# Perceiver block on one core: expert weights summed by accumulating DMAs, the key split on GpSimd, all query copies on ScalarE, new instruction orders

## The chip, the cores and the metric

The kernel runs on one core of one Trainium2 chip. Its engines are TensorE (PE; PEld are its weight loads), VectorE (DVE), ScalarE (ACT), GpSimd (POOL) and SyncE (SP, which here only issues DMAs). The metric is the device time of one execution in microseconds (us).

## What is computed

A batch of 64 x 64 tokens of width 128 goes through a cross attention on a context, a causal attention over binary trees, and a layer of product-key experts, each with a layer norm ahead and a residual sum behind.

```python
def reference(x, ctx_768, ...):
    x = x + _L0_xattn_ref(_layernorm(x), ctx_768, Wq, Wk, Wv, Wo, bo)   # 16 heads of 64
    x = x + _L0_attn_ref(_layernorm(x), Wp, bp, Wv, Wo)                 # 16 heads, tree depth 5
    x = x + _L0_ffn_ref(_layernorm(x), Wq, bq, K1, K2, W_up, W_down)    # 8 heads, 32 x 32 keys, top 10
    return x

def _L0_ffn_ref(x, ...):
    q = (x @ Wq + bq).reshape(B, S, N_HEADS, D_QUERY)
    s1, s2 = einsum(q[..., :16], K1), einsum(q[..., 16:], K2)
    v1, i1 = top_k(s1, 10); v2, i2 = top_k(s2, 10)
    vals, best = top_k((v1[..., :, None] + v2[..., None, :]).reshape(..., 100), 10)
    expert_idx = take_along_axis(i1[..., :, None] * 32 + i2[..., None, :], best)
    scores = softmax(vals)
    h = gelu(einsum('bsd,bshkd->bshk', x, W_down[expert_idx])) * scores
    return einsum('bshk,bshkd->bsd', h, W_up[expert_idx])
```

## The kernel before, in words

**Tiles.** The tokens are cut into 32 tiles of 128 (two sequences each). Every tile goes through over 100 steps; a step has a name such as `x.s0` and is a handful of instructions of one engine. The prefix tells the part: `x.` and `y.` are the cross attention, `t.` the tree attention, `k.` the keys, `e.` the experts.

**Order.** Each engine runs through `for i in range(NT + depth)` and, in each iteration, through its own table (`PE_ORDER`, `ACT_ORDER`, `DVE_ORDER`, `POOL_ORDER`, `SP_ORDER`) from first name to last. The number at a name is its lag: in iteration `i` the step works on tile `i - lag`, so that about five tiles are under way at once. An engine never leaves its table's order: what waits holds up all behind it. Between engines every step waits on semaphores, one for each name (`s[name]`, counted per tile). `BANK` says in which bank of PSUM a step of PE writes: x0, x1, t0, t1 are single banks, f0 and f1 are double ones that the experts use in turn.

**Cross attention.** `x.norm` (POOL) and `x.turn` (PE) give the transposed input; `x.q0` to `x.q3` make the queries of four heads each, `x.w0` to `x.w3` copy them to SBUF (L622 on ACT, `x.w3` L626 on DVE); `x.s0` to `x.s3` are the scores, `x.x` their maxima (DVE), `x.e` the exponentials (ACT, L694), `x.r` the reciprocals (DVE), `x.n` the scaling (POOL, L1057), `x.p` the transposes, `x.t` their copies, `y.m` the mixes, `y.u` their copies, `y.out` the projection, and `y.res` the residual sum with the statistics of the next layer norm (DVE, L893).

**Trees.** `t.norm` (POOL, L1044 and L1047), `t.turn`, `t.sb`, `t.pv`, `t.pexp`, `t.path`, `t.feat` (POOL), `t.fturn`, `t.fsb`, `t.sim`, `t.exp`, `t.mix`, `t.div`, `t.cturn`, `t.csb`, `t.out`, `t.res`: one dependent chain over all engines.

**Keys.** `k.norm`, `k.turn`, `k.high`/`k.low`, then `k.key` gives the scores of 16 x 32 keys. `k.top` (DVE) takes the eight largest of each key list and subtracts the largest in place in PSUM. `k.split` (DVE, L950 and L952) writes the shifted scores as two float16 parts into `us`; `k.kturn` (SP) turns `us` with a transposing DMA into `usT`. `k.shift` (ACT, L755) copies the shifted scores into `cand`; in this kernel it waits for `k.split`. `k.inner` (POOL) adds the inner candidates. `k.cand` (DVE, three groups of eight) finds the threshold, `k.cut` (POOL) its middle, `k.eb`, `k.z` and `k.lnz` the logarithm of the softmax's sum.

**Experts.** For each of 8 heads `h`, `e.s<h>` (PE, L589) expands `usT` to the sums of all 1024 experts, `e.x<h>` (ACT, L784) takes their exponential, `e.w<h>` (DVE, L996) masks it into one of four slots of `mw`. `e.a1` to `e.a7` (POOL, L1117) add the eight masked arrays one after another into `wsum`, 128 x 1024 float32 each. `e.wturn` transposes `wsum`, `e.hid` and `e.gelu` are the hidden values, with an activation table loaded before and after the Gelu, `e.gate` (DVE, L1007) multiplies the two, `e.out` and `e.add` finish the tile.

**Setup.** Some products of weights are made once: `setup_vo` on PE ahead of the first `x.s0`, `setup_keys` on PE ahead of the first `x.p1`. Their weights lie in buffers of their own.

## Time and profile before

| | us |
|---|---|
| median of 3 runs | 1101.47 |
| lowest and highest | 1100.77 and 1102.71 |
| the profiled execution's own time | 1100.73 |
| its span | 1097.8 |
| busy PE, share of the span | 980.3, 89% |
| busy POOL | 892.2, 81% |
| busy DVE | 876.6, 80% |
| busy ACT | 873.4, 80% |

The profiled execution lies 0.7 us under the median. The busy times are sums over the whole span; PE's matmuls are pipelined and their ends are modelled, so that its busy share is an upper estimate of its work. All four engines are busy for most of the span, and none for all of it. Except for the filling and the emptying of the pipeline the program repeats one iteration, so its trace is best read as one period.

### The profile page before, as it was taken

To read this page: it belongs to the slowest core of one execution; us is meant where nothing else is said; L and a number is where in the kernel's file an instruction comes from. 1 tells how busy PE (TensorE), PEld (TensorE's weight loads), DVE (VectorE), ACT (ScalarE), POOL (GpSimd) and SP (SyncE) were. 2 spreads that over 40 slices of the span, in tenths; PEclk is the share of its full clock that TensorE was granted. 3 is DMA by queue.
4 is the path that set the end of the run, shared out by engine and by line. 5 is a ranking of instruction groups with operands and counts; after the bars stand their busy time and mean duration, and the time that the engine had idled before them with its cause. 6 is when DMAs were issued, how large, how long until landed. Compare 5 with 4: busy or idle time off the path is not lost. (4 is left out here: it accounts for less than half of the span.)

```text
span 1097.8 us, 35846 instructions
## 1 busy us (share of the span) xinstructions
PE 980.3 (89%) x12440; PEld 778.7 (71%) x12440; DVE 876.6 (80%) x2877; ACT 873.4 (80%) x2127; POOL 892.2 (81%) x935
## 2 busy tenths in 40 slices
PE   6879899999999999999999999999999999999765
PEld 5667677777777777777777777777777777777533
DVE  3267888888888888888888888888888888888773
ACT  3548888888888888888988888888888888988652
POOL 1327888898888888988888898888888988888765
PEclk9979999999999999999999999999999999999876
DMA  6000011110100111100011110100111100010000
GB/s 166 14 19 17 12 26 26 26 26 20 24 16 20 27 25 26 26 20 14 20 26 26 26 26 20 24 14 23 26 26 26 25 21 15 20 24 20 14 13 5
DMA packets 70367, 27.25 MB, mean 25 GB/s; under 512 B 47312, under 2 KB 69936, under 8 KB 70192
## 3 DMA queue, kind: packets, MB, share of 16 engines
q1 hardware_dynamic: 69152, 24.58, 9.6%
q8 instruction: 103, 1.69, 0.6%
q14 instruction: 72, 0.59, 0.2%
q10 hardware_dynamic: 1040, 0.39, 0.1%
HBM read 14.47 MB, written 2.10 MB: 15 GB/s over the span
## 5 line engine op out<-in xcount | busy, mean ns | idle before, releaser
L1117 POOL TENSOR_TENSOR wsum<-wsum,mw 128x1024 f32<-128x1024 f32 x192 | 452.8, 2358 | 5.5
L996 DVE SCALAR_TENSOR_TENSOR mw<-psF,cut,ew 128x1024 f32<-128x1024 f32 x256 | 324.9, 1280 | 46.0 <-ACT ew L784 46.0
L784 ACT ACTIVATE ew<-psF,lnz 128x1024 f32<-128x1024 f32 x256 | 280.9, 1124 | 12.5 <-PE psF L589 9.7
L1057 POOL TENSOR_TENSOR p<-p,rrow 128x512 f32<-128x512 f32 x128 | 131.5, 1038 | 94.0 <-DVE rrow L882 94.0
L694 ACT ACTIVATE p<-psXT,negmax 128x128 f32<-128x128 f32 x512 | 181.4, 383 | 2.2 <-DVE negmax L873 2.2
L589 PE MATMUL psF<-sel,usT 128*128 128x512 f16 x512 | 158.8, 394 | 18.0 <-DVE mw L996 16.6
L377 PEld LDWEIGHTS psXT<-cT,q 96*128 96x128 f32 x1024 | 131.4, 194 | 54.8 <-DVE q L626 39.8
L377 PE MATMUL psXT<-cT,q 96*128 96x128 f32 x1024 | 142.3, 283 | 27.7 <-DVE q L626 25.6
L694 ACT ACTIVATION_READ_ACCUMULATOR p<-psXT,negmax 128x1 f32 x512 | 115.4, 225 | 0.0
L873 DVE TENSOR_REDUCE negmax<-psXT 128x4 f32<-128x512 f32 x128 | 85.9, 671 | 35.3 <-PE psXT L377 35.3
L418 PE MATMUL psXT<-pT,c 128*32 128x384 f32 x768 | 104.4, 499 | 0.7 <-ACT pT L622 0.7
L420 PE MATMUL psXT<-pT,c 128*32 128x128 f32 x768 | 102.5, 277 | 0.0
L312 PE MATMUL psXT<-xnT,qk 128*96 128x128 f16 x512 | 91.1, 222 | 3.4 <-DVE xnT L864 1.8
L439 PE MATMUL psXT<-vo,uT 128*128 128x128 f32 x768 | 92.6, 277 | 0.0
L1047 POOL TENSOR_SCALAR xn<-x,mv,rstd 128x128 f32<-128x128 f32 x96 | 76.9, 801 | 17.3 <-POOL rstd L1044 17.3
L313 PE MATMUL psXT<-xnT,qk 128*96 128x128 f16 x512 | 90.7, 221 | 0.0
L314 PE MATMUL psXT<-xnT,qk 128*96 128x128 f16 x512 | 90.7, 221 | 0.0
L439 PEld LDWEIGHTS psXT<-vo,uT 128*128 128x128 f32 x768 | 88.3, 192 | 0.0
L1044 POOL TENSOR_TENSOR rstd<-mv,halfneg 128x1 f32<-128x1 f32 x96 | 54.2, 564 | 37.1 <-DVE mv L850 34.6
L755 ACT ACTIVATE cand<-psXT 128x512 f32<-128x512 f32 x32 | 19.1, 597 | 80.9 <-DVE us L952 80.9
L1117 POOL TENSOR_TENSOR wsum<-mw 128x1024 f32<-128x1024 f32 x32 | 75.6, 2361 | 8.9 <-DVE mw L996 8.9
L622 ACT ACTIVATE pT<-psXT 128x512 f32<-128x512 f32 x128 | 74.1, 605 | 9.6 <-PE psXT L396 8.8
(133 smaller groups left out, 2359.7 us busy)
## 6 DMA issues: line engine op xcount, KB each, us to landing
cT<-cT_dram SPq DMA_DIRECT2D x32, 96.0 KB, 2.0
c<-c_dram SPq DMA_DIRECT2D x32, 96.0 KB, 2.1
x<-x_dram SPq DMA_DIRECT2D x32, 64.0 KB, 2.3
xr<-x_dram SPq DMA_DIRECT2D x32, 64.0 KB, 1.8
y_dram<-y SPq DMA_DIRECT2D x32, 64.0 KB, 1.6
wqT<-wqT_dram SPq DMA_DIRECT2D x1, 512.0 KB, 5.0
wo<-wo_dram SPq DMA_DIRECT2D x1, 512.0 KB, 6.2
wdT<-wdT_dram SPq DMA_DIRECT2D x1, 512.0 KB, 3.5
```

What stands on the lines that cost most here:

```text
L312: pe.matmul(out, left[:, 0, :], right[:, 0, :], start=not open_group, stop=False)
L313: pe.matmul(out, left[:, 0, :], right[:, 1, :], start=False, stop=False)
L377: mm = pe.matmul(bank[BANK[f"x.s{k}"]][:, i * M:i * M + M], q[:, b, h:h + 2, :].rearrange("c h q -> c (h q)"), cT[:, t % 2, b, :], start=T ...
L418: pe.matmul(to[32 * j:32 * j + 32], cols, probs[:, :, 0:3, :], start=True, stop=True, tile_position=(0, 32 * j))
L420: mm = pe.matmul(to[96:128, :, j, :], cols, probs[:, :, 3, :], start=True, stop=True, tile_position=(0, 96))
L439: mm = pe.matmul(out, uT[:, i, :, :].rearrange("c b q -> c (b q)"), vo[:, i, :], start=False, stop=(i == XH3 - 1))
L589: mm = pe.matmul(bank[BANK[f"e.s{h}"]][:, j * 512:j * 512 + 512], usT[:, t % 4, h, :], sel[:, j * 512:j * 512 + 512], start=True, stop=True)
L694: ins = act.activation(p[:, k, i, :], bank[BANK[f"x.s{k}"]][:, i * M:i * M + M], ACT.Exp, bias=negmax[:, k, i:i + 1], accum_out=rowsum[:, ...
L784: done(f"e.x{h}", act.activation(ew[:, h % NEW, :], bank[BANK[f"e.s{h}"]], ACT.Exp, bias=lnz[:, t % 4, h:h + 1]))
L996: done(f"e.w{h}", dve.scalar_tensor_tensor(out=mw[:, h % NMW, :], in0=bank[BANK[f"e.s{h}"]], scalar=cut[:, t % 4, h:h + 1], in1=ew[:, h % ...
L1057: done(f"x.n{k}", pool.tensor_tensor(p[:, k, :, :], p[:, k, :, :], rrow[:, k, :].unsqueeze(2).to_broadcast([128, 4, M]), ALU.mult))
L1117: done(f"e.a{h}", pool.tensor_tensor(wsum[:, t % 2, :], mw[:, 0, :] if h == 1 else wsum[:, t % 2, :], mw[:, h % NMW, :], ALU.add))
```

## The change

The change has five parts.

1. **Sums of the weights.** `mw` has twelve slots where it had four (`slot(t, h)` walks round them). Six of the seven additions leave POOL's arithmetic: three accumulating DMAs, issued by POOL (`e.sa`, `e.sb`, `e.sc`), each add two neighbouring slots (128 x 2048 float32, 1 MB) onto the tile's first two. Each waits for the one before to land. `e.fin` adds the last two slots on POOL into `wsum`. POOL itself waits where a DMA has to have landed.
2. **Key split.** `k.split` moves from DVE (two instructions from PSUM) to POOL (three instructions from `cand`). So it now waits for `k.shift`, and `k.shift` waits for `k.top` only.
3. **Query copies.** `x.w3` moves from DVE to ACT.
4. **Setup.** `setup_vo` now stands ahead of the first `x.p0` and `setup_keys` ahead of the first `t.turn`; their weights are loaded into `mw` slots 5 to 11, which are free until tile 0 or 1 masks into them. `setup_vo` has one wait for all its products on ACT where it had four.
5. **New tables.** All five orders and the banks are new, with the semaphore waits for the banks that follow from them. All lags but those of a few steps at the table's ends are one less; the distances between steps are about the same.

```diff
-NEW, NMW = 4, 4
+LOWEST = -16.0
+NEW, NMW = 4, 12
+SUMS = ("e.sa", "e.sb", "e.sc")
...
+        mw = sb("mw", [128, NMW, NE])
+
+        def early(i, at, parts, n):
+            return mw[0:128, i, at:at + parts * n].rearrange("p (h d) -> p h d", h=parts)
+
+        wdT = mw[:, 5, :]
+        fwqT, fbqT, keys = early(6, 0, 2, D), early(6, 256, 2, 96), early(6, 512, 4, 2 * NSQ)
...
+        def slot(t, h):
+
+            return (FH * t + h) % NMW
...
             def w_turn(t):
-                after(pe, "e.w3", t + 1)
+                after(pe, "e.w0", t + 1)
                 at_ends(pe, "e.add", t - 1)
-                pe.wait_ge(s[f"e.a{FH - 1}"], t + 1)
+                pe.wait_ge(s["e.fin"], t + 1)
...
             def shifted(t):
-                act.wait_ge(s["k.split"], t + 1)
+                act.wait_ge(s["k.top"], t + 1)
                 after(act, "k.cand", t - 2)
+                after(act, "k.split", t - 2)
...
-            def split(t):
-                dve.wait_ge(s["k.top"], t + 1)
-                after(dve, "k.kturn", t - 1)
-                lsp.begin(t)
-                uh = bank[BANK["k.key"]].rearrange("p (h i) -> p h i", h=FH)
-                lsp.link(dve.tensor_scalar_max(us[:, :, 0, :], uh, FLOOR))
-                lsp.wait()
-                done("k.split", dve.scalar_tensor_tensor(out=us[:, :, 1, :], in0=uh, scalar=FLOOR, in1=us[:, :, 0, :],
-                                                         op0=ALU.max, op1=ALU.subtract))
...
-                    if h < NMW:
-                        after(dve, f"e.a{h + FH - NMW}", t - 1)
-                    else:
-                        dve.wait_ge(s[f"e.a{max(h - NMW, 1)}"], t + 1)
-                    done(f"e.w{h}", dve.scalar_tensor_tensor(out=mw[:, h % NMW, :], in0=bank[BANK[f"e.s{h}"]],
+
+                    after(dve, ("e.sb", "e.sc", "e.fin", "e.sa")[h // 2], t - (2 if h < 4 else 1))
+                    done(f"e.w{h}", dve.scalar_tensor_tensor(out=mw[:, slot(t, h), :], in0=bank[BANK[f"e.s{h}"]],
...
+            def split(t):
+
+                pool.wait_ge(s["k.shift"], t + 1)
+                after(pool, "k.kturn", t - 1)
+                lsp.begin(t)
+                pool.nop(nofuse=True)
+                scores = cand[:, t % 2, :, 0:2 * NSQ]
+                lsp.link(pool.tensor_scalar_max(us[:, :, 0, :], scores, FLOOR))
+                lsp.wait()
+                lsp.link(pool.tensor_tensor(rest[:], scores, us[:, :, 0, :], ALU.subtract))
+                lsp.wait()
+                done("k.split", pool.tensor_scalar_max(us[:, :, 1, :], rest[:], LOWEST))
+            steps["k.split"] = split
...
-                    done(f"e.a{h}", pool.tensor_tensor(wsum[:, t % 2, :],
-                                                       mw[:, 0, :] if h == 1 else wsum[:, t % 2, :],
-                                                       mw[:, h % NMW, :], ALU.add))
...
+            def add_pairs(name, h, before):
+
+                def step(t):
+                    for i in range(h if before else 0, h + 2):
+                        pool.wait_ge(s[f"e.w{i}"], t + 1)
+                    if before:
+                        pool.wait_ge(s[before], 16 * (t + 1))
+                    pool.nop(nofuse=True)
+                    to, by = slot(t, 0), slot(t, h)
+                    pool.dma_start(mw[:, to:to + 2, :], mw[:, by:by + 2, :], accum_op=ALU.add).then_inc(s[name], 16)
+                return step
+            steps["e.sa"] = add_pairs("e.sa", 2, None)
+            steps["e.sb"] = add_pairs("e.sb", 4, "e.sa")
+            steps["e.sc"] = add_pairs("e.sc", 6, "e.sb")
+
+            def add_last(t):
+                pool.wait_ge(s["e.sc"], 16 * (t + 1))
+                after(pool, "e.wturn", t - 2)
+                done("e.fin", pool.tensor_tensor(wsum[:, t % 2, :], mw[:, slot(t, 0), :], mw[:, slot(t, 1), :], ALU.add))
+            steps["e.fin"] = add_last
...
 POOL_ORDER = {
-    "e.a7": 6, "k.cut": 5, "x.norm": 2, "t.feat": 4, "x.n0": 3, "x.n2": 3, "e.a1": 5, "x.n1": 3, "x.n3": 3,
-    "e.a2": 5, "k.norm": 4, "e.a3": 5, "e.a4": 5, "e.a5": 5, "k.inner": 4, "e.a6": 5, "t.norm": 3,
+    "e.sc": 5, "k.cut": 4, "t.feat": 3, "x.norm": 1, "x.n0": 2, "e.fin": 5, "e.sa": 4, "x.n2": 2, "x.n1": 2,
+    "x.n3": 2, "k.norm": 3, "e.sb": 4, "k.inner": 3, "k.split": 3, "t.norm": 2,
 }
...
-PE_VO = "x.s0"
-PE_KEYS = "x.p1"
+PE_VO = "x.p0"
+PE_KEYS = "t.turn"
```

**POOL, second half of an iteration, before.** From `k.norm` to `k.cut`; the name in brackets is the semaphore that a row waits for (`e_a5` is the fifth addition, `y_res` the residual sum that `t.norm` needs).

```order
L1047 TENSOR_SCALAR xn<-x,mv,rstd 128x128 [waits pool_k_norm]
L1117 TENSOR_TENSOR wsum<-wsum,mw 128x1024 [waits e_w3,e_a2]
L1117 TENSOR_TENSOR wsum<-wsum,mw 128x1024 [waits e_w4,e_a3]
L1117 TENSOR_TENSOR wsum<-wsum,mw 128x1024 [waits e_w5,e_a4]
L1069 TENSOR_TENSOR tops<-top 128x80 [waits k_cand,k_top]
L1075 TENSOR_TENSOR cand<-tops 128x8x4 [waits pool_inner]
L1117 TENSOR_TENSOR wsum<-wsum,mw 128x1024 [waits e_w6,e_a5]
L1044 TENSOR_TENSOR rstd<-mv,halfneg 128x1 [waits t_turn,y_res]
L1047 TENSOR_SCALAR xn<-x,mv,rstd 128x128 [waits pool_t_norm]
L1117 TENSOR_TENSOR wsum<-wsum,mw 128x1024 [waits e_w7,e_a6]
L1087 TENSOR_TENSOR cut<-best 128x8 [waits k_cand,e_w7]
```

The same place after.

```order
L1047 TENSOR_SCALAR xn<-x,mv,rstd 128x128 [waits pool_k_norm]
L1132 DMA mw<-mw 128x2048 [waits e_sa,e_w4,e_w5]
L1069 TENSOR_TENSOR tops<-top 128x80 [waits k_cand,k_top]
L1075 TENSOR_TENSOR cand<-tops 128x8x4 [waits pool_inner]
L1088 TENSOR_SCALAR us<-cand 128x8x64 [waits k_shift,k_kturn]
L1090 TENSOR_TENSOR rest<-cand,us 128x512 [waits pool_split]
L1092 TENSOR_SCALAR us<-rest 128x8x64 [waits pool_split]
L1044 TENSOR_TENSOR rstd<-mv,halfneg 128x1 [waits t_turn,y_res]
L1047 TENSOR_SCALAR xn<-x,mv,rstd 128x128 [waits pool_t_norm]
L1132 DMA mw<-mw 128x2048 [waits e_sb,e_w6,e_w7]
L1101 TENSOR_TENSOR cut<-best 128x8 [waits k_cand,e_w7]
```

Five additions have gone from this stretch, two DMA issues (`e.sb`, `e.sc`) and the split stand in their place, and `t.norm` has the split ahead of it and no addition.

**DVE, end of an iteration, before:** from the maxima of the keys to the first group of `k.cand`.

```order
L941 TENSOR_TENSOR psXT<-psXT,top 128x512 [waits dve_top]
L864 TENSOR_TENSOR xnT<-psXT,xnT 128x128 [waits x_high,x_turn]
L950 TENSOR_SCALAR us<-psXT 128x8x64 [waits k_kturn,k_top]
L952 SCALAR_TENSOR_TENSOR us<-psXT,us 128x8x64 [waits dve_split]
L996 SCALAR_TENSOR_TENSOR mw<-psF,cut,ew 128x1024 [waits e_a3,k_cut,e_x7]
L893 TENSOR_TENSOR x<-xr,psXT 128x128 [waits t_norm,ld_xr,y_out]
```

The same place after.

```order
L954 TENSOR_TENSOR psXT<-psXT,top 128x512 [waits dve_top]
L996 SCALAR_TENSOR_TENSOR mw<-psF,cut,ew 128x1024 [waits e_sa,k_cut,e_x6]
L877 TENSOR_TENSOR xnT<-psXT,xnT 128x128 [waits x_high,x_turn]
L858 BN_STATS st<-x 128x6 [waits x_norm,ld_x]
L861 BN_AGGR mv<-st 128x2 [waits dve_x_stats]
L906 TENSOR_TENSOR x<-xr,psXT 128x128 [waits t_norm,ld_xr,y_out]
```

The two instructions of the split are gone, and `x.stats` has come here from the first half of the iteration.

## Rows read from the trace of the kernel before

**Rows 1.** Busy time by stretch: engine, us busy (instructions), granted clock, DMA share, GB/s.
```profile
400.00:600.00 200.00, 185.41 (x2383) 148.18 (x2383) 170.32 (x555) 170.55 (x422) 174.46 (x187) 1.00 0.10 23
```

**Rows 2.** Timeline of DVE (start, duration): the same mask, `e.w2`, one iteration apart.
```profile
500.09 2.47 DVE L996 SCALAR_TENSOR_TENSOR mw<-psF,cut,ew 128x1024 f32<-128x1024 f32 x2 [0.23 <-ACT ew L784]
...
531.73 2.48 DVE L996 SCALAR_TENSOR_TENSOR mw<-psF,cut,ew 128x1024 f32<-128x1024 f32 x2 [0.23 <-ACT ew L784]
```

**Rows 3.** Groups by line: count, busy us and mean ns, idle before and releaser.
```profile
L1117 POOL TENSOR_TENSOR wsum<-wsum,mw 128x1024 f32<-128x1024 f32 x192 | 452.8, 2358 | 5.5
L1057 POOL TENSOR_TENSOR p<-p,rrow 128x512 f32<-128x512 f32 x128 | 131.5, 1038 | 94.0 <-DVE rrow L882 94.0
L622 ACT ACTIVATE q<-psXT 96x512 f32<-96x512 f32 x96 | 53.1, 590 | 9.0 <-PE psXT L314 8.6
```

**Rows 4.** Timeline of DVE in that iteration, from the gate to `k.cand`.
```profile
507.94 1.22 DVE L1007 TENSOR_TENSOR gT<-psF,gh 128x1024 f32<-128x1024 f32 x1 [0.51 <-PE psF L601]
...
519.33 0.68 DVE L950 TENSOR_SCALAR us<-psXT 128x512 f16<-128x512 f32 x1
...
521.86 0.29 DVE L893 TENSOR_TENSOR x<-xr,psXT 128x128 f32<-128x128 f32 x1
...
523.00 1.18 DVE L965 MAX8 best<-cand 128x8 f32<-128x72 f32 x8
...
526.10 1.18 DVE L975 MAX8 best<-cand 128x8 f32<-128x72 f32 x8
```

**Rows 5.** Timeline of ACT in that iteration.
```profile
504.32 1.12 ACT L784 ACTIVATE ew<-psF,lnz 128x1024 f32<-128x1024 f32 x1
505.31 0.38 ACT L694 ACTIVATE p<-psXT,negmax 128x128 f32<-128x128 f32 x1
...
506.68 1.04 ACT L733 ACTIVATE am<-psXT 128x1024 f32<-128x1024 f32 x1
...
520.77 0.60 ACT L755 ACTIVATE cand<-psXT 128x512 f32<-128x512 f32 x1 [2.43 <-DVE us L952]
```

**Rows 6.** Timeline of POOL at the end of that iteration.
```profile
522.50 2.36 POOL L1117 TENSOR_TENSOR wsum<-wsum,mw 128x1024 f32<-128x1024 f32 x1
524.81 0.56 POOL L1044 TENSOR_TENSOR rstd<-mv,halfneg 128x1 f32<-128x1 f32 x1
```

**Rows 7.** Timeline of PE in that iteration.
```profile
506.81 1.09 PE L601 MATMUL psF<-ident,wsum 128*128 128x128 f32 x8
507.87 1.12 PE L504 MATMUL psXT<-v,am 64*64 64x9 f32 x64
...
511.56 0.51 PE L418 MATMUL psXT<-pT,c 128*32 128x384 f32 x1
...
521.98 2.05 PE L611 MATMUL psF<-wup,gT 128*128 128x128 f32 x16 [0.15 <-DVE mw L996]
```

**Rows 8.** DMA issues: KB each and median us from issue to landing.
```profile
cT<-cT_dram SPq DMA_DIRECT2D x32, 96.0 KB, 2.0
...
wdT<-wdT_dram SPq DMA_DIRECT2D x1, 512.0 KB, 3.5
...
usT<-us SPq DMA_TRANSPOSE x32, 3.0
```

**Rows 9.** Timeline of SP: what the issue of a DMA takes.
```profile
520.83 1.23 SPq L226 DMA_TRANSPOSE usT<-us  x1
523.04 0.33 SPq L200 DMA_DIRECT2D xr<-x_dram  x1
```

**Rows 10.** Timeline of PE in the first iteration, from `setup_vo` to `x.s0`.
```profile
16.87 0.67 PE L284 MATMUL psF<-wo,wvT 64*96 64x128 f32 x6
...
22.37 2.05 PE L377 MATMUL psXT<-cT,q 96*128 96x128 f32 x16
```

**Rows 11.** Timeline of POOL in the last iteration.
```profile
1072.56 2.35 POOL L1117 TENSOR_TENSOR wsum<-mw 128x1024 f32<-128x1024 f32 x1 [6.08 <-DVE mw L996]
1074.98 14.47 POOL L1117 TENSOR_TENSOR wsum<-wsum,mw 128x1024 f32<-128x1024 f32 x6
```

140 lines of the change are left out of this document (63 added, 77 removed), and 23 rows, old and new, of tables (ACT_ORDER, BANK, PE_ORDER).

## The prediction

> **What bounds the kernel now.** I read the busy times by stretch first, then the timelines of one iteration, engine by engine, then the first and last iteration. In the middle of the run no engine is full: of 200 us PE is busy for 185, POOL 174, ACT 171 and DVE 170, with PE's clock at its full 2.4 GHz [rows 1]. One mask returns after 531.73 - 500.09 = 31.64 us [rows 2], which is the period P. In it PE works 29.3 us (185.4 / 200 x 31.64), POOL 27.6, ACT 27.0, DVE 26.9. What sets P is therefore a ring of waits through fixed orders, and two waits in it are seen plainly. ACT stands idle for 2.43 us ahead of the copy `k.shift` until DVE has finished the split [rows 5]. And the statistics for `t.norm` are ready at about 522.95, as `k.cand` starts at 523.00 right behind them [rows 4], but POOL is in an addition from 522.50 and starts `t.norm` at 524.81 [rows 6]: 1.9 us late, at the head of the long tree chain.
>
> **Loads after the change.** POOL loses six additions of 2.36 us [rows 3], 14.2 us an iteration, and gets the split and three DMA issues. The split's three instructions have 512 elements each; the two-input row of that size takes 1.04 us [rows 3]. Bounds are 1.0 us (one such instruction, the others hidden) and 7.1 us (each as long as an addition); I take 2.6, with the one-input ones at 0.8. An issue costs 0.33 us on SP for a plain DMA and 1.23 for the transposing one [rows 9]; GpSimd's accumulating one is not in this trace, and I take 1.0, nearer to the one with the more involved descriptors. POOL comes to 27.6 - 14.2 + 2.6 + 3.0 = 19.0. DVE loses 0.68 + 0.7 for the split [rows 4] and about 0.7 for `x.w3`: 24.8. ACT gains one query copy of 0.59 [rows 3]: 27.6. PE's matmuls stay: 29.3, an upper estimate of its work. So the floor falls nowhere by more than a little, and the gain can only come from the ring.
>
> **The new ring.** The split leaves the path: from 519.33, when DVE starts it, to 520.77, when `k.shift` starts, are 1.44 us [rows 4, 5]. `t.norm` starts up to 1.9 us earlier, if the split on POOL is done by then. Both come before the same next iteration, so that they don't add. I laid the new tables out with the durations of the rows, and the longest ring that is left goes once round in one period:
> - `y.res` with statistics 1.14 (521.86 to 523.00) and `k.cand` 4.28 (523.00 to the end of the second-last row's eight maxima, 527.28) [rows 4]: 5.4
> - on ACT twelve steps in a row, from `k.eb` to `t.exp`: four `e.x` and the like-sized `t.fsb` at 0.99 (504.32 to 505.31), two `x.e` at 1.37 (505.31 to 506.68), `t.exp` 1.04 [rows 5], a query copy 0.59 [rows 3], three small ones at about 0.25: 10.1
> - on PE `t.mix` and `e.wturn`, 1.12 + 1.06 [rows 7]: 2.2
> - on DVE the gate, 1.22 [rows 4]
> - on PE from `e.s4` to the end of `y.out`. Before, from 511.56 to 521.83 (521.98 less the 0.15 idle) the same steps but one `x.p` and one `e.s` took 10.3 [rows 7]; with half of the 1.06 of eight transposes and about 0.4 for these: 11.2
> - five hand-overs at about 0.1: 0.5
>
> The sum is 30.5 (5.4 + 10.1 + 2.2 + 1.2 + 11.2 + 0.5 = 30.6, rounded down for what overlaps). DVE is nearly full at the end of it: `e.w6`, `x.low`, `x.stats` come right ahead of `y.res`, so that what POOL gives up isn't the next thing late. P falls by 31.64 - 30.5 = 1.1. There are 29 full iterations ((1030 - 100) / 31.64): **-33 us**. The bounds are P = 29.6, near PE's 29.3 (-59 us), and P = 31.6, where another hand-over takes what these gave back (0).
>
> **The DMAs.** A 96 KB load lands in 2.0 us, the 512 KB one in 3.5 [rows 8]: 3.6 ns a KB, and 5.3 us for 1 MB. An accumulation also reads its destination; counted as a second MB that makes 9.0. The bounds are thus 5.3 and 9.0, and I take the middle, L = 7.2, as the second MB is read and not written. POOL waits only where it must: `e.sa` is issued right behind `e.fin`, each next one after the landing. The ring `e.fin`, `e.sa`, `e.sb`, `e.sc`, `e.fin` needs 2.36 + 3 x (L + 1.0) = 27.0 us, less than 30.5, and the DMAs are hidden. It decides from L plus issue = 9.4. The Trainium skill, "DMA: Bandwidth & Descriptors", section "Anatomy of one DMA — SWDGE (gpsimd) path", fits about 2.0 us plus bytes at 436 GB/s, and its "Collectives: The Full Stack" says that a reducing DMA needs two source reads, which halves its rate: 2.0 + 2 x 2.4 = 6.8 us, by estimate, and the sum below would be 1 us lower. The same DMA page gives GpSimd's path about 1 us to the first byte. No run here shows either yet.
>
> With twelve slots no mask waits for a slot: `e.w4` needs the `e.fin` of the tile before, some 6 us earlier. `k.kturn` has less room. `k.top` ends about 2.1 us ahead of the end of `y.out`; with the copy (0.6), the split (2.6) and 3.0 to landing [rows 8] the keys are there 4.1 us behind it, and `e.s1` is due at 5.2 (seven PE steps behind `y.out`). That hides the split now, with 1.1 us to spare; beyond it each us is paid for.
>
> **Start and end.** `setup_vo` stood on PE from 16.87 to 22.37 ahead of the first scores [rows 10]: 5.5 us. It now runs ahead of `x.p0`, where PE waits for POOL and ACT anyway; I take -4, between 0 and -5.5. At the end nothing hides the DMAs. Before, the seven additions of the last tile ran from 1072.56 to 1089.45 [rows 11]. After, `e.sa` waits for the fourth mask, one mask (1.2) later than the first addition did: 1073.8 + 3 x 8.2 + 2.4 = 1100.8. That is **+11 us** (+4 with 5.3 and 0.33, +17 with 9.0 and 1.23).
>
> **Sum.** Against the profiled execution's own 1100.7 us (span 1097.8; 0.7 below the median of 1101.5): -33 - 4 + 11 = -26, 1075 us; on the median's scale the same within 1 us.
>
> **The rivals.**
> 1. *The sums' ring becomes the period (slower).* Place: POOL's waits ahead of `e.sb`, `e.sc` and `e.fin`, with `k.inner`, `k.split`, `t.norm` and `k.cut`, `t.feat` queued behind. With L = 9.0 and issue 1.23 the ring takes 2.36 + 3 x 10.2 = 33.1: 29 x 1.4 = +42, end +17, start -4, 1156 us. It decides against the gain from L plus issue = 9.4 and makes the kernel slower from about 9.6. For it: nothing in the trace shows an accumulating DMA. Against it: the middle of the bounds is 1.2 us under the point.
> 2. *The keys come late (no change or slower).* The split at 4.6 us instead of 2.6, or `k.kturn` at 5 us because it shares the DMA engines with `e.sb` and `e.sc`, uses the 1.1 us and takes 1 us more of every period; `t.norm` behind the split is late by as much. P is 31.5: 1100.7 - 4 + 7 = 1104 us.
> 3. *The ring is shorter than my sum.* If the orders overlap more than I saw, PE's 29.3 is next: P = 29.6, 1100.7 - 59 - 4 + 11 = 1049 us.
> 4. *The sums don't leave the path.* If GpSimd is held for an issue by as long as the DMA itself, POOL's load is 19 + 3 x 6 = 37 us a period, and the time is over 1250.
>
> **Chances.** Forecast (P from 30.0 to 31.1, 1058 to 1094) 0.60; rival 1, 0.14; rival 2, 0.13; rival 3, 0.08; rival 4, 0.05. The likeliest time is 1075. The range takes in rival 2 and half of rival 3: 1050 to 1125. A difference below 0.2% (2.2 us) can't be told from none here. Faster by over 0.2%: forecast, rival 3 and a third of rival 2, 0.73. Within 0.2%: 0.04. Slower: rivals 1 and 4 and most of rival 2, 0.23.
>
> **What would show each step.** P from one mask to the same one 29 iterations on: 30.5. `k.shift` without idle time for DVE's split; POOL in `t.norm` within 0.3 us of the statistics. `mw` DMAs landing in 5.3 to 9.0 us and POOL waiting under 2 us an iteration for them. L1088 to L1092 at 2.6 us together. In the last iteration some 25 us between the fourth mask and `e.fin`. The first `x.s0` at about 17 us. The forecast is wrong if POOL waits for DMAs ahead of `k.split`, if PE waits for `usT` ahead of `e.s1`, or if the masks' own rows (2.48 us for two, [rows 2]) grow longer beside the DMA traffic.

## The result, and the profile after

The changed kernel takes 1139.35 us (median of 4 runs, 1137.57 to 1142.78), the one before 1101.87 in the same comparison (1100.77 to 1102.71): a ratio of 1.0345, interval 1.0316 to 1.0373. The forecast was 1075 with a range of 1050 to 1125, so the sign was wrong and the time lies outside the range. The profiled execution of the changed kernel took 1140.48 us, with a span of 1138.6.

First the busy times of the stretch that [rows 1] show for the kernel before (columns as there):

```profile
400.00:600.00 200.00, 182.12 (x2412) 147.58 (x2410) 158.35 (x551) 172.52 (x413) 130.67 (x182) 1.00 0.60 122
```

POOL went from 174 to 131 us of 200, DVE from 170 to 158 and ACT from 171 to 173, as the new loads demand. And PE does less in the same time, 182 instead of 185. No engine is nearer to full than PE was, so some ring of waits became longer. The DMA share went from 0.10 to 0.60.

Where the 40.8 us of span came from is read from one instruction that each tile has once, the subtraction of `k.top` on DVE:

| stretch | before | after | difference |
|---|---|---|---|
| start to tile 0's `k.top` | 73.2 | 76.9 | +3.6 |
| tile 0 to tile 3 | 96.6 | 101.4 | +4.8 |
| tile 3 to tile 30 (27 periods) | 855.5 | 868.9 | +13.3 |
| tile 30 to tile 31 | 32.9 | 32.9 | 0 |
| last `k.top` to the end | 39.5 | 58.6 | +19.0 |

The regular period is 31.88 us (31.64 before). The mean of the 27 is 32.18, since four of them take 33.5. The forecast was 30.5.

One regular iteration of the changed kernel, POOL's timeline around the split and `t.norm` (start, duration, engine, line; in brackets the idle time before and what ended it); before, `t.norm` began at 524.81 [rows 6]:

```profile
500.79 1.49 POOL L1088 TENSOR_SCALAR us<-cand 128x512 f16<-128x512 f32 x1
502.37 1.15 POOL L1090 TENSOR_TENSOR rest<-cand,us 128x512 f32<-128x512 f32 x1
503.61 1.48 POOL L1092 TENSOR_SCALAR us<-rest 128x512 f16<-128x512 f32 x1
505.17 0.58 POOL L1044 TENSOR_TENSOR rstd<-mv,halfneg 128x1 f32<-128x1 f32 x1
505.93 0.80 POOL L1047 TENSOR_SCALAR xn<-x,mv,rstd 128x128 f32<-128x128 f32 x1 [0.18 <-POOL rstd L1044]
506.68 0.92 POOL L1132 DMA_DIRECT2D mw<-mw  x1
```

Its three engines around it, from the timelines of DVE, PE and ACT:

```profile
503.00 0.15 DVE L863 TENSOR_SCALAR mv<-mv 128x1 f32<-128x1 f32 x1
503.20 0.91 DVE L967 MAX8 best<-cand 128x8 f32<-128x72 f32 x6
```
```profile
506.88 0.30 PE L462 MATMUL psXT<-ident,xn 128*128 128x128 f32 x1 [1.67 <-POOL xn L1047]
```
```profile
507.22 0.28 ACT L717 ACTIVATE xn2T<-psXT 128x128 f32<-128x128 f32 x1 [2.74 <-PE psXT L462]
507.39 1.20 ACT L632 ACTIVATE q<-psXT 96x512 f32<-96x512 f32 x2
508.55 0.28 ACT L730 ACTIVATE v<-psXT 128x128 f32<-128x128 f32 x1
508.73 0.26 ACT L776 ACTIVATE ebest<-best 128x80 f32<-128x80 f32 x1
```

The split takes from 500.79 to 505.09, 4.3 us. The statistics that `t.norm` needs are ready at 503.15, and it starts at 505.17: 2.0 us late, as late as before the change (1.9). PE then waits 1.67 us and ACT 2.74, and `k.eb` (L776), which opens ACT's long run, comes at 508.73, behind the tree's copies in ACT's order.

The last tile, from the timelines of SP, PE, DVE and POOL:

```profile
1086.31 1.23 SPq L235 DMA_TRANSPOSE usT<-us  x1
```
```profile
1095.88 1.86 PE L599 MATMUL psF<-sel,usT 128*128 128x512 f16 x4 [11.86 <-DMA usT<-us]
```
```profile
1098.08 2.48 DVE L996 SCALAR_TENSOR_TENSOR mw<-psF,cut,ew 128x1024 f32<-128x1024 f32 x2 [11.09 <-ACT ew L798]
```
```profile
1086.27 0.90 POOL L1132 DMA_DIRECT2D mw<-mw  x1
...
1104.69 0.89 POOL L1132 DMA_DIRECT2D mw<-mw  x1 [5.10 <-DVE mw L996]
1112.27 0.86 POOL L1132 DMA_DIRECT2D mw<-mw  x1 [6.68 <-DMA mw<-mw]
1119.82 0.86 POOL L1132 DMA_DIRECT2D mw<-mw  x1 [6.69 <-DMA mw<-mw]
1126.85 2.33 POOL L1141 TENSOR_TENSOR wsum<-mw 128x1024 f32<-128x1024 f32 x1 [6.17 <-DMA mw<-mw]
```

Two things are to be seen. The chain of the three DMAs is 7.6 us from one issue to the next, and from the first mask to the end it is 40.5 us (29.8 before, where the first mask of the last tile began at 1068.05): +10.8, where the forecast had 11. And the transposing DMA of the keys was issued 0.04 us behind an accumulating one and landed only after some 9.4 us, when the median is 3.1. That, with the longer split, is the other 8.3 us of the end, and the forecast had none of it. Rival 2 names a late `k.kturn` beside the accumulating DMAs, but for the regular period. In e3_thin below, whose accumulating DMAs are cut to 16 KB, the last keys go out 0.03 us behind one of them and land after 3.3 us: it is the length of the DMA ahead that counts, and not its issue. From the DMA view of the end, 1070 to 1138 us of the changed kernel and 1080 to 1138 us of e3:

```profile
usT<-us SPq DMA_TRANSPOSE x1, 9.4
```
```profile
usT<-us SPq DMA_TRANSPOSE x1, 3.3
```

### The profile page after: what moved, and what is told of

Read it like the earlier page. It is cut to its first block, busy times and chain, and to the rows that moved or that the text cites. A ratio compares the mean times of both kernels' runs of the same rounds, so it can differ in the third digit from the quotient of the medians.

```text
span 1138.6 us, 35745 instructions
## 1 busy us (share of the span) xinstructions
PE 976.5 (86%) x12440; PEld 780.0 (69%) x12440; DVE 817.8 (72%) x2781; ACT 891.0 (78%) x2155; POOL 669.9 (59%) x935
## 4 chain that ended last, share of the span: by engine, by line
POOL 38%; PE 22%; issue 15%; DVE 15%; ACT 6%; DMA 3%; POOLq 1%; ACTq 0%; SPq 0%; DVEq 0%
POOL wsum L1141 6%; POOL feat L1115 5%; PE psXT L406 5%; DVE top L951 5%; POOL us L1088 4%; POOL us L1092 4%; POOL xn L1047 4%; DVE mw L996 4%; ACT ew L798 4%; PE psXT L428 3%; POOL rest L1090 3%; POOL p L1057 3%; POOL rstd L1044 3%; PE psF L599 3%; POOL mw L1132 2%
## 5 line engine op out<-in xcount | busy, mean ns | idle before, releaser
L599 PE MATMUL psF<-sel,usT 128*128 128x512 f16 x512 | 161.7, 400 | 41.1 <-DVE mw L996 27.9
L1057 POOL TENSOR_TENSOR p<-p,rrow 128x512 f32<-128x512 f32 x128 | 139.2, 1237 | 67.4 <-DVE rrow L895 67.4
L1132 POOL DMA_DIRECT2D mw<-mw x96 | 89.3, 930 | 124.3 <-DMA mw<-mw 94.1
L707 ACT ACTIVATION_READ_ACCUMULATOR p<-psXT,negmax 128x1 f32 x512 | 112.2, 219 | 0.0
L428 PE MATMUL psXT<-pT,c 128*32 128x384 f32 x768 | 111.7, 505 | 0.4 <-ACT pT L632 0.4
L430 PE MATMUL psXT<-pT,c 128*32 128x128 f32 x768 | 109.5, 280 | 0.0
L322 PE MATMUL psXT<-xnT,qk 128*96 128x128 f16 x512 | 97.8, 227 | 2.7 <-DVE mv L863 1.5
L323 PE MATMUL psXT<-xnT,qk 128*96 128x128 f16 x512 | 97.5, 226 | 0.0
L324 PE MATMUL psXT<-xnT,qk 128*96 128x128 f16 x512 | 97.5, 226 | 0.0
L406 PE MATMUL psXT<-ident,p 128*128 128x128 f32 x512 | 83.4, 288 | 10.7 <-POOL p L1057 10.7
L632 ACT ACTIVATE q<-psXT 96x512 f32<-96x512 f32 x128 | 75.5, 591 | 16.4 <-PE psXT L324 12.7
L599 PEld LDWEIGHTS psF<-sel,usT 128*128 128x128 f16 x512 | 48.8, 104 | 57.9 <-DVE mw L996 40.4
```

The lines of the kernel that those rows point to most:

```text
L406: mm = pe.transpose(bank[BANK[f"x.p{k}"]][:, i * 128:i * 128 + 128], p[:, k, i, :], ident[:])
L428: pe.matmul(to[32 * j:32 * j + 32], cols, probs[:, :, 0:3, :], start=True, stop=True, tile_position=(0, 32 * j))
L599: mm = pe.matmul(bank[BANK[f"e.s{h}"]][:, j * 512:j * 512 + 512], usT[:, t % 4, h, :], sel[:, j * 512:j * 512 + 512], start=True, stop=True)
L707: ins = act.activation(p[:, k, i, :], bank[BANK[f"x.s{k}"]][:, i * M:i * M + M], ACT.Exp, bias=negmax[:, k, i:i + 1], accum_out=rowsum[:, ...
L1057: done(f"x.n{k}", pool.tensor_tensor(p[:, k, :, :], p[:, k, :, :], rrow[:, k, :].unsqueeze(2).to_broadcast([128, 4, M]), ALU.mult))
L1132: pool.dma_start(mw[:, to:to + 2, :], mw[:, by:by + 2, :], accum_op=ALU.add).then_inc(s[name], 16)
```

## The experiments

Theory: the loss is the split on GpSimd, 4.3 us and not 2.6, with `t.norm` behind it, and at the end the DMA chain and the late keys. First rival: the accumulating DMAs, which keep the DMA engines 60% busy and make the loads land later (`x` after 7.5 us instead of 2.3), slow the kernel. Second rival: PE's own work and small waits hold every full kernel at 31.5. Names with `e` and `f` start from the changed kernel, those with `p` from the one before. The time is the median of a kernel's runs in us, its ratio that to the kernel before as measured beside it (its medians there lie from 1101.9 to 1104.9). The other columns are read from the profiled execution: "period" is the commonest distance of two `k.top`, "mean" the mean from tile 3 to tile 30. e3 and e8 leave out part of the work and only serve to answer a question.

| kernel | time | ratio to before | first `k.top` | period | mean | last `k.top` to end |
|---|---|---|---|---|---|---|
| before | 1101.9 | 1 | 73.2 | 31.64 | 31.69 | 39.5 |
| after | 1139.4 | 1.0345 | 76.9 | 31.88 | 32.18 | 58.6 |
| e1_tnorm_first | 1394.7 | 1.2632 | 71.4 | 40.6 | 40.64 | 58.1 |
| e2_split_dve | 1125.0 | 1.0196 | 71.6 | 31.62 | 32.18 | 50.1 |
| e3_thin | 1141.0 | 1.0312 | 78.7 | 32.26 | 32.62 | 42.6 |
| p1_sums_only | 1109.9 | 1.0029 | 74.0 | 31.51 | 31.65 | 50.6 |
| e6_tail | 1120.5 | 1.0163 | 71.1 | 31.92 | 32.16 | 44.1 |
| e8_half_split | 1085.6 | 0.9831 | 73.9 | 30.70 | 30.78 | 50.3 |
| p4_sums_split_late_tail | 1087.0 | 0.9846 | 73.9 | 31.01 | 31.30 | 40.4 |
| p5_sums_tail | 1100.5 | 0.9972 | 74.3 | 31.53 | 31.73 | 39.3 |
| f1_dve_first_tail | 1097.8 | 0.9969 | 78.6 | 31.26 | 31.60 | 41.3 |
| f2_shared_tail | 1093.6 | 0.9925 | 78.6 | 31.14 | 31.40 | 39.7 |
| f3_tnorm_first_sc_late | 1278.8 | 1.1609 | 71.6 | 36.95 | 37.02 | 52.3 |
| f4_vo_first_tail | 1125.6 | 1.0205 | 76.0 | 31.88 | 32.23 | 44.1 |

### The size of the split: e8_half_split

```diff
-                scores = cand[:, t % 2, :, 0:2 * NSQ]
-                lsp.link(pool.tensor_scalar_max(us[:, :, 0, :], scores, FLOOR))
+                g = FH // 2
+                scores = cand[:, t % 2, 0:g, 0:2 * NSQ]
+                lsp.link(pool.tensor_scalar_max(us[:, 0:g, 0, :], scores, FLOOR))
...
-                lsp.link(pool.tensor_tensor(rest[:], scores, us[:, :, 0, :], ALU.subtract))
+                lsp.link(pool.tensor_tensor(rest[:, 0:g], scores, us[:, 0:g, 0, :], ALU.subtract))
...
-                done("k.split", pool.tensor_scalar_max(us[:, :, 1, :], rest[:], LOWEST))
+                done("k.split", pool.tensor_scalar_max(us[:, 0:g, 1, :], rest[:, 0:g], LOWEST))
```

> The changed kernel with the split on GpSimd cut to 4 of its 8 heads (the other half of us is set to zero once; the keys of those heads are left out of the work of the split only, everything behind it runs in full). Theory A (the step that failed is the split's price, 4.3 us instead of 2.6, which keeps t.norm waiting 2.0 us behind the ready statistics): the split takes 2.2 to 2.4 us, t.norm starts when y.res is done, PE's wait for it falls from 1.67 to under 0.5 us, the period goes to 30.6 to 30.8 as the prediction's ring had it, and 29 periods give 1139 - 34 = 1105, less if the longer iterations go too. Theory B (TensorE's own 29 us and the waits in between hold the period at 31.5, as in the two kernels without a split on GpSimd, 31.51 and 31.62): the period stays at 31.5 or more, 1128 or more.

Measured: 1085.55 us, ratio 0.9831 (0.9792 to 0.9871), period 30.70. POOL's and ACT's timelines of a regular iteration:

```profile
507.64 0.85 POOL L1090 TENSOR_SCALAR us<-cand 128x256 f16<-128x256 f32 x1
508.58 0.67 POOL L1092 TENSOR_TENSOR rest<-cand,us 128x256 f32<-128x256 f32 x1
509.34 0.85 POOL L1094 TENSOR_SCALAR us<-rest 128x256 f16<-128x256 f32 x1
510.27 0.58 POOL L1045 TENSOR_TENSOR rstd<-mv,halfneg 128x1 f32<-128x1 f32 x1
```
```profile
514.36 0.27 ACT L776 ACTIVATE ebest<-best 128x80 f32<-128x80 f32 x1 [0.41 <-DVE best L977]
```

The run leaves out the split of four of the eight heads. The split took 2.55 us, almost the 2.6 of the forecast, and the period is the forecast's unrounded sum, 30.6, within 0.1. `k.eb` now waits for `k.cand` on DVE, the step that the ring names. Behind the end of `y.res` it starts 4.4 us later (510.00 to 514.36), in the changed kernel 5.6 us (503.15 to 508.73). The difference, 1.2 us, is that of the periods, 31.88 - 30.70. So theory A holds, and the second rival, a floor at 31.5, falls. The time is 20 us under the expected 1105, as the longer iterations went too. The accumulating DMAs were in full use here (a share of 0.63), so that the first rival has nothing left in the regular period either. Of the 58.8 us of span between this run and the changed kernel, 37.7 lie between tiles 3 and 30, 8.0 between tiles 0 and 3, 8.3 in the end, where the keys now went out 0.6 us ahead of the accumulating DMA, 1.9 between the last two tiles, and 3.0 at the start, where the two profiles differ in PE's clock (see the setup below).

### The split on VectorE: e2_split_dve, f1_dve_first_tail, f2_shared_tail

```diff
+            def split(t):
+                dve.wait_ge(s["k.shift"], t + 1)
+                after(dve, "k.kturn", t - 1)
+                lsp.begin(t)
+                uh = cand[:, t % 2, :, 0:2 * NSQ]
+                lsp.link(dve.tensor_scalar_max(us[:, :, 0, :], uh, FLOOR))
+                lsp.wait()
+                done("k.split", dve.scalar_tensor_tensor(out=us[:, :, 1, :], in0=uh, scalar=FLOOR, in1=us[:, :, 0, :],
+                                                         op0=ALU.max, op1=ALU.subtract))
...
-    "x.n3": 2, "k.norm": 3, "e.sb": 4, "k.inner": 3, "k.split": 3, "t.norm": 2,
+    "x.n3": 2, "k.norm": 3, "e.sb": 4, "k.inner": 3, "t.norm": 2,
```

In e2 it stands in DVE's table between `y.res` and `k.cand`, in f1 ahead of `y.res`. In f2 GpSimd writes the upper half in one instruction and VectorE the lower one between `y.res` and `k.cand`. f1 and f2 also have the end of e6 (below).

> The changed kernel with the key split back on DVE (two instructions, read from cand behind k.shift, placed between y.res and k.cand), nothing of it on POOL. Theory A (the split on POOL is the ring): t.norm starts within 0.3 us of its statistics, the keys' DMA starts about 0.6 us earlier than in the changed kernel, k.cand 1.4 us later; period 30.7 to 31.3, 1105 to 1122. Theory B (the DMAs' ring): period within 0.1 us of 31.89, about 1139.

> The changed kernel with the split on VectorE ahead of y.res (two instructions, 0.43 and 0.69 us where the run with the split behind y.res showed them), and the last tile's sums on GpSimd and VectorE as in e6. Ring theory (PE's y.m1, y.res, k.cand, ScalarE's run, masks, PE back to y.m1: 30.7 us with nothing else in it, as the run with half a split showed, 31.6 with the split between y.res and k.cand): VectorE had 0.41 us idle ahead of y.res, so the split adds 1.06 - 0.41 = 0.65 to the ring, period 31.3; with the end of e6 that is 1125 - 31 x 0.3 - 12 = 1103, down to 1090 if the iterations of 32.8 us at the lower clock go too. Floor theory (PE's own work and small waits keep any full kernel at 31.5): period 31.6, 1110 or more.

> The changed kernel with the split shared: GpSimd writes the upper half (one instruction, 1.49 us, ends before y.res is ready, so t.norm is not late), VectorE the lower half between y.res and k.cand (one of 0.69 us), the end as in e6. Ring theory: 30.7 + 0.6 = 31.3, time 1090 to 1103 as for the kernel with both on VectorE ahead of y.res. Floor theory: 31.5 or more, 1110. If GpSimd's one instruction were enough to make t.norm late: 31.9 and 1120, as e6.

Measured: e2 1125.02 us (ratio 1.0139 to 1.0252), period 31.62; f1 1097.79 (0.9953 to 0.9985), 31.26; f2 1093.63 (0.9902 to 0.9948), 31.14. In e2's DVE timeline the two instructions and the maxima behind them:

```profile
494.39 0.43 DVE L963 TENSOR_SCALAR us<-cand 128x512 f16<-128x512 f32 x1
494.85 0.69 DVE L965 SCALAR_TENSOR_TENSOR us<-cand,us 128x512 f16<-128x512 f32 x1
495.46 1.17 DVE L978 MAX8 best<-cand 128x8 f32<-128x72 f32 x8
```

What the split adds to the way from `y.res` to `k.cand` is seen in the period: 1.07 us there, and e2 has 30.70 + 0.92; 0.41 of it hidden in a wait of DVE, f1 has 30.70 + 0.56; only the lower half, f2 has 30.70 + 0.44 (0.6 was expected). In all three the period grows by what was put into the forecast's ring, less 0.1 to 0.25 us. e2's expectation, 30.7 to 31.3 and at most 1122 us, was missed: it had `k.cand` later by the split, and put that cost too low. e2 gains 14 us on the changed kernel, but its mean period is no better, since 11 of its iterations took about 32.8 us. Busy time by stretch for two iterations of e2 that follow each other:

```profile
554.62:586.24 31.62, 29.30 (x390) 23.35 (x388) 26.05 (x88) 27.65 (x67) 16.96 (x26) 1.00 0.59 119
586.24:619.04 32.80, 30.71 (x390) 24.35 (x387) 26.30 (x89) 27.86 (x67) 17.05 (x26) 0.95 0.60 122
```

The same 390 matmuls take 1.4 us longer, and the granted clock is 0.95 instead of 1.00, at half speed for part of the iteration. The four long iterations of the changed kernel are of this kind too, for instance this one and the next:

```profile
337.89:371.36 33.47, 30.41 (x389) 24.82 (x387) 25.14 (x86) 27.65 (x67) 20.89 (x29) 0.95 0.52 104
371.36:403.26 31.90, 28.93 (x390) 23.34 (x387) 25.15 (x87) 27.52 (x67) 21.00 (x29) 1.00 0.67 134
```

Between 344 and 346 us PE had worked for 0.34 us, with a wait of 1.66; it ran at half clock from about 347.5 to 351. But the same wait, 1.66 or 1.67 us, stands in each of the other iterations too, and most of them keep the full clock. The kernels in which PE has one wait of 1.2 to 1.7 us on average in each iteration (after, e2, e3, e6, f1, f2, f4) have 3 to 11 iterations that are about 1 us or more too long. Where the longest of PE's regular waits is 0.8 to 1.0 us there are none (before, e8) or one or two (p1, p4, p5). The two go together, but no run here changed the wait alone.

### The keys' DMA and the accumulating DMA: e1_tnorm_first, f3_tnorm_first_sc_late

```diff
-    "x.n3": 2, "k.norm": 3, "e.sb": 4, "k.inner": 3, "k.split": 3, "t.norm": 2,
+    "x.n3": 2, "k.norm": 3, "e.sb": 4, "k.inner": 3, "t.norm": 2, "k.split": 3,
```

That is e1. f3 has it too, and `e.sc` behind `t.feat`:

```diff
-    "e.sc": 5, "k.cut": 4, "t.feat": 3, "x.norm": 1, "x.n0": 2, "e.fin": 5, "e.sa": 4, "x.n2": 2, "x.n1": 2,
+    "k.cut": 4, "t.feat": 3, "e.sc": 5, "x.norm": 1, "x.n0": 2, "e.fin": 5, "e.sa": 4, "x.n2": 2, "x.n1": 2,
```

> The changed kernel with two neighbours in POOL's table swapped: t.norm now ahead of k.split. In the changed kernel the period is 31.89 us, and t.norm starts at 505.17, 2.0 us behind its statistics (503.15), because the split is in front of it; PE then idles 1.67 us ahead of t.turn. Theory A (the split on POOL, in front of t.norm, is what sets the period): t.norm 2 us earlier, the keys' DMA 1.5 us later, which costs some of it back at e.s1; period 30.6 to 31.3, whole time 1100 to 1125. Theory B (the ring of the three accumulating DMAs sets it): period stays within 0.1 us of 31.89, 1137 to 1142.

> The changed kernel with t.norm ahead of the split, as in e1 (1394.7 us, period 40.6), but with the accumulating DMA e.sc behind t.feat instead of at the split's end, so that the transposing DMA of the keys is issued 3 us ahead of it and not 0.04 us behind it. Theory A (e1 was slow since the transposing DMA behind an accumulating one landed after 6.7 us instead of 3.1): it lands after 3.1 to 3.5 us, PE's wait for the keys falls from 8.8 to about 5 us, period 36 to 37, time 1240 to 1270. Theory B (the later split alone makes e1 slow): period above 39, time above 1350.

Measured: e1 1394.72 us (ratio 1.256 to 1.2703), f3 1278.79 (1.1567 to 1.1652). e1 was meant to bring `t.norm` forward, and it did; it made the kernel 255 us slower than the changed one. One iteration of e1, from the timelines of POOL, SP and PE, and the DMA view's row for the keys (median us to landing):

```profile
485.76 0.95 POOL L1132 DMA_DIRECT2D mw<-mw  x1
```
```profile
485.80 1.24 SPq L235 DMA_TRANSPOSE usT<-us  x1
```
```profile
492.59 1.01 PE L599 MATMUL psF<-sel,usT 128*128 128x512 f16 x2 [8.83 <-DMA usT<-us]
493.40 1.92 PE L387 MATMUL psXT<-cT,q 96*128 96x128 f32 x8
```
```profile
usT<-us SPq DMA_TRANSPOSE x5, 6.8
```

The split ends just as `e.sc` is issued, in each iteration, and the transposing DMA behind the accumulating one lands after 6.8 us. PE stands for 8.83 us, and the eight score products behind take 1.92 us instead of the 1.06 they take at full clock. In f3, where the accumulating DMA goes out 3 us behind, the same rows read:

```profile
493.10 1.01 PE L599 MATMUL psF<-sel,usT 128*128 128x512 f16 x2 [5.24 <-DMA usT<-us]
```
```profile
usT<-us SPq DMA_TRANSPOSE x5, 3.1
```

The landing is back at 3.1, and 3.7 us of landing gave 3.65 of period (40.6 to 36.95): theory A, to the size, though the time is 9 us above its 1270. The other 5.1 us above the changed kernel's 31.88 stand behind the keys, which the split gives 4.1 us later (from the start of `k.inner` to the split's end 9.5 us instead of 5.4); the first products behind PE's wait run at half clock here too (1.01 us instead of 0.59), and how the 5.1 us divide between the two is not measured. The prediction's sentence on `k.kturn`, "beyond it each us is paid for", is what the 3.7 us show.

### The DMAs' size: e3_thin

```diff
-                    pool.dma_start(mw[:, to:to + 2, :], mw[:, by:by + 2, :], accum_op=ALU.add)
+                    pool.dma_start(mw[:, to:to + 2, 0:16], mw[:, by:by + 2, 0:16], accum_op=ALU.add)
```

The accumulating DMAs add 16 of 1024 columns; the other columns of six of the eight weights are left out of the sum.

> The changed kernel with its three accumulating DMAs a tile cut to 16 of 1024 columns of each slot (so the weights of the other 1008 experts lack six of the eight heads); all waits and issues stay. Takes away the DMAs' length and traffic. Theory A (the split on POOL sets the period): period stays near 31.9; only the end becomes shorter, by 3 x about 5 us for the last tile's sums and about 6 us for the last keys' DMA: 1115 to 1125. Theory B (the DMAs' ring or their traffic): POOL's 2.7 us of waiting for DMAs go and the period falls to 31 or below, 1095 or less.

Measured: 1141.03 us (ratio 1.0243 to 1.0382), the time of the changed kernel, which neither theory expected. The landing fell to 2.6 us and the DMA share to 0.14, but the period rose to 32.26: the narrow DMA costs POOL 1.27 us of issue instead of 0.93, and one of the issues stands ahead of `x.n`. From the groups by line, 300 to 900 us, of e3 and of the changed kernel:

```profile
L1132 POOL DMA_DIRECT2D mw<-mw x56 | 71.0, 1269 | 46.9 <-DVE mw L996 37.8 <-issue 9.0
```
```profile
L1132 POOL DMA_DIRECT2D mw<-mw x56 | 52.2, 931 | 61.1 <-DMA mw<-mw 51.9 <-issue 8.3 <-DVE mw L996 0.7
```

PE's waits for `x.n` in that stretch (total, times, longest), again of e3 and of the changed kernel:

```profile
PE psXT L406 <- POOL p L1057: 13.6, 19, 1.8
```
```profile
PE psXT L406 <- POOL p L1057: 6.7, 18, 1.1
```

That is 0.35 us more a period, and the period rose by 0.38. e3 thus has a cost of its own, and it is this sum, not the time alone, that leaves nothing for the traffic or for POOL's 2.7 us of waiting for a landing (51.9 / 19). Together with e8, which reaches the forecast's ring with the DMAs in full use, it lets the first rival fall. Where the landing counts is the end: 42.6 us instead of 58.6. The 16 us won there went into the longer middle (+11.8 from tile 3 to 30), the tiles before (+2.6) and the start (+1.8).

### The sums alone, and the end: p1_sums_only, p5_sums_tail, e6_tail

p1 is the kernel before with the accumulating DMAs, the twelve slots and the setup weights loaded into them, and nothing else of the change; DVE, ACT and PE keep the tables of before:

```diff
-NEW, NMW = 4, 4
+NEW, NMW = 4, 12
...
-    "e.a7": 6, "k.cut": 5, "x.norm": 2, "t.feat": 4, "x.n0": 3, "x.n2": 3, "e.a1": 5, "x.n1": 3, "x.n3": 3,
-    "e.a2": 5, "k.norm": 4, "e.a3": 5, "e.a4": 5, "e.a5": 5, "k.inner": 4, "e.a6": 5, "t.norm": 3,
+    "e.sc": 6, "k.cut": 5, "x.norm": 2, "t.feat": 4, "e.fin": 6, "x.n0": 3, "x.n2": 3, "e.sa": 5, "x.n1": 3, "x.n3": 3,
+    "k.norm": 4, "e.sb": 5, "k.inner": 4, "t.norm": 3,
```

p5 and e6 are p1 and the changed kernel with another end: GpSimd adds the pairs 2+3 and 4+5 of the last tile, VectorE the rest behind the last mask, and the last accumulating DMA waits for the last keys.

```diff
+                    to, by = slot(t, 0), slot(t, h)
+                    if t == NT - 1:
+                        if h == 4:
+                            pool.wait_ge(own["pool_last"], 1)
+                        if h < 6:
+                            pool.tensor_tensor(mw[:, to:to + 2, :], mw[:, to:to + 2, :], mw[:, by:by + 2, :], ALU.add)\
+                                .then_inc(own["pool_last"], 1)
+                        return
...
+                    if t == NT - 2 and h == 6:
+                        pool.wait_ge(s["k.kturn"], 16 * NT)
...
+                if t == NT - 1:
+                    m = [mw[:, slot(t, h), :] for h in (0, 1, 6, 7)]
...
+                    dve.tensor_tensor(m[2], m[2], m[3], ALU.add).then_inc(own["dve_last"], 1)
+                    dve.wait_ge(own["pool_last"], 2)
+                    dve.tensor_tensor(m[0], m[0], m[1], ALU.add).then_inc(own["dve_last"], 1)
+                    dve.wait_ge(own["dve_last"], 2)
+                    after(dve, "e.wturn", t - 2)
+                    done("e.fin", dve.tensor_tensor(wsum[:, t % 2, :], m[0], m[2], ALU.add))
```

> The kernel before with the first part of the change alone: twelve slots, three accumulating DMAs and one addition instead of seven additions on POOL; orders of the other engines, key split on DVE, x.w3 on DVE and setup as before. Theory A (the DMAs are hidden; what they free on POOL lets t.norm start 1.9 us earlier): period 31.0 to 31.6 against 31.69, end about 11 to 18 us longer (serial DMAs of the last tile), so 1095 to 1115. Theory B (the DMAs' ring or traffic slows each iteration): period 32 or more, 1125 or more.

> The kernel before with the accumulating sums alone, but the last tile's sums on GpSimd and VectorE. In the run without this end the period was 31.51 (31.64 before) and the end after the last k.top 50.6 us (39.5 before). Theory A: the chain of three DMAs was the whole of these 11 us; the last sum is ready 12 us earlier, the end is 38 to 40 us, 1097 to 1099. Theory B: the sums' end was hidden behind other work, 1107 or more.

> The changed kernel, but the last tile's sums use no accumulating DMA: pairs 2+3 and 4+5 are added on GpSimd, 6+7 and the final sum on VectorE; and the last accumulating DMA of the tile before waits until the last tile's transposing DMA has landed. Theory A (the end is long because of the chain of three accumulating DMAs, 7.5 us from issue to issue, and because the last transposing DMA stood right behind one and took 9.4 us instead of 3.1): transposing DMA 3.1 us, first mask of the last tile 6 us earlier, the last sum ready about 12 us after that first mask's adds instead of 29, so the end after the last k.top falls from 58.6 us to about 40 and the time to 1139 - 18 = 1121. Theory B (the end is long for the clock or for PE's own work): under 5 us are gained, 1135 or more. Both: the period stays 31.88.

Measured: p1 1109.91 us (ratio 0.9997 to 1.006), p5 1100.51 (0.995 to 0.9994), e6 1120.50 (1.0119 to 1.0208). Taking 14 us of additions from POOL gives p1 only 0.13 us a period, and costs it 11.1 at the end; p5 gets the end back (39.3 us, where the kernel before has 39.5), though not the 1097 to 1099 that were expected. p1 shows two things more, here a row of POOL's timeline and the keys' row of the DMA view from 400 to 600 us:

```profile
522.98 0.57 POOL L1045 TENSOR_TENSOR rstd<-mv,halfneg 128x1 f32<-128x1 f32 x1 [2.70 <-DVE mv L854]
```
```profile
usT<-us SPq DMA_TRANSPOSE x6, 5.2
```

`t.norm` waits there until its statistics are ready, where it was 1.9 us late before. So those 1.9 us, which the prediction calls plainly seen as a wait in the ring, were worth at most 0.13 us a period in the old orders. And the keys land after 5.2 us instead of 3.0, as in that stretch they are issued 4.4 to 5.9 us behind an accumulating DMA, which takes 8 us to land; PE has no wait for them from 300 to 900 us, so that here it costs nothing.

e6's end is 44.1 instead of 58.6. Its last transposing DMA, and the accumulating one that now waits for it (in the changed kernel PE waited 11.86 us for these keys):

```profile
1079.45 1.23 SPq L235 DMA_TRANSPOSE usT<-us  x1
```
```profile
1083.16 0.90 POOL L1156 DMA_DIRECT2D mw<-mw  x1 [3.80 <-DMA usT<-us]
```

It landed after 3.1 us, and the accumulating DMA went out 3.7 us behind its issue. The end was expected at 40 and is 44. The first mask of the last tile starts 11.6 us behind its `k.top` (9.8 in the kernel before), and the next masks stand in DVE's order behind the gate of the tile before, whose `e.fin` comes only at 1090.22; that the time is nevertheless the expected 1121 is owed to the start, 5.8 us shorter in this profile (see the setup below).

### Setup: f4_vo_first_tail

```diff
-PE_VO = "x.p0"
-ACT_VO = "x.t0"
+PE_VO = "x.s0"
+ACT_VO = "x.e0"
```

f4 also has the end of e6.

> The changed kernel with the products of setup_vo back in front of tile 0's scores (PE ahead of x.s0, ScalarE ahead of x.e0), the end as in e6. In e6 the products stand ahead of x.p0 and tile 0's k.top starts at 71.1 us, in the profile of the changed kernel, whose products ran at half the clock, at 76.9. Theory A (moving them hides about half of their 5.5 us when the clock stays up): first k.top at 73 to 76 at full clock, time 2 to 4 us above e6, 1122 to 1125. Theory B (what they hide behind waits for them later, nothing is won): first k.top at 71, time that of e6, 1120. Both: period 31.9.

Measured: 1125.61 us (1119.31 to 1131.75), e6 1120.50 (1119.22 to 1131.41): the two overlap, and the time decides nothing. The first `k.top` came at 76.0, which is theory A's upper edge, but not at full clock. Busy time from 25 to 30 us and from 30 to 35, first of the changed kernel, then of e6, which has the same instructions there:

```profile
25.00:30.00 5.00, 5.00 (x26) 3.35 (x25) 0.18 (x1) 0.93 (x6) 1.75 (x2) 0.50 0.00 0
30.00:35.00 5.00, 5.00 (x25) 3.67 (x24) 0.00 (x0) 1.27 (x4) 0.00 (x0) 0.50 0.00 0
```
```profile
25.00:30.00 5.00, 4.88 (x44) 3.59 (x40) 0.18 (x1) 1.74 (x7) 1.60 (x2) 1.00 0.00 0
30.00:35.00 5.00, 3.83 (x49) 2.79 (x51) 0.00 (x0) 3.82 (x9) 0.00 (x0) 1.00 0.09 23
```

At half clock (1.2 GHz) PE's products take 10 us instead of 5.5 and the first `k.top` comes at 76.9, at full clock at 71.1. Of the nine profiles with the products at their new place four have them at half clock (76.9, 78.6, 78.6, 78.7), four at full clock with the first `k.top` at 71.1 to 71.6, and one (e8, 73.9) has them at full clock but half clock from about 52 to 67 us. The four that keep the old place in the old orders have 73.2 to 74.3, and f4, with the old place in the new orders, has the half clock from 30 to 35 us. So the new start is 2 us shorter when the clock holds and 3 to 5 longer when it doesn't; what the place of the products gives by itself is not shown, as f4 has no profile at full clock. What decides between the clocks stays open.

### Sums, a later split and the short end: p4_sums_split_late_tail

```diff
-                act.wait_ge(s["k.split"], t + 1)
+                act.wait_ge(s["k.top"], t + 1)
...
+                after(act, "k.split", t - 2)
...
-                dve.wait_ge(s["k.top"], t + 1)
+                dve.wait_ge(s["k.shift"], t + 1)
...
-                uh = bank[BANK["k.key"]].rearrange("p (h i) -> p h i", h=FH)
+                uh = cand[:, t % 2, :, 0:2 * NSQ]
...
-    "e.w4": 5, "t.res": 4, "e.w5": 5, "k.low": 4, "e.w6": 5, "k.top": 4, "x.low": 2, "k.split": 4, "e.w7": 5,
+    "e.w4": 5, "t.res": 4, "e.w5": 5, "k.low": 4, "e.w6": 5, "k.top": 4, "x.low": 2, "e.w7": 5, "k.split": 4,
```

This is p5 with ACT's copy ahead of DVE's split; the split reads the copy and stands behind the last mask.

> The kernel before with the accumulating sums, the key split on VectorE behind the last mask from the copied scores (ScalarE's k.shift waits for k.top alone), and the last tile's sums on GpSimd and VectorE. Theory A (ScalarE's 2.4 us of waiting for the split before k.shift lie off the ring): the period stays 31.5, and with the end as in p5 the time is that of p5, 1097. Theory B (they are in the ring): the period falls to 30.5 to 31.0, 1070 to 1082.

Measured: 1086.96 us, ratio 0.9846 (0.9818 to 0.9873), against 1100.51 for p5. The period is 31.01, at the upper edge of theory B's 30.5 to 31.0; the time is 5 us above its 1082, as the mean period is 31.30. ACT's waits between 300 and 900 us (total, times, longest), first of p5, then of p4:

```profile
ACT cand L759 <- DVE us L956: 46.4, 19, 2.7
```
```profile
ACT cand L760 <- DVE psXT L946: 17.7, 19, 1.1
```

ACT's 2.4 us ahead of the copy were in the ring, as the prediction said, and 0.5 us of the period was to be had for them with the orders of before. (The split moved by one place too; the two were not tried apart.) This version does all the work and beats both kernels, and its two parts beyond the sums are these few lines and the end of the last tile.

No run tests the move of `x.w3` or the new orders by themselves.

## Why the prediction was wrong, step by step

- **The step that failed is the price of the split**, "I take 2.6, with the one-input ones at 0.8". It measured 1.49 + 1.15 + 1.48 with its gaps, 4.3 us, inside the stated bounds of 1.0 and 7.1. The two-input instruction was right (1.04 taken, 1.15 measured). The one-input ones were taken as cheaper than the two-input one for no row's sake. The trace before had a one-input row that speaks against it, `t.norm`'s own, 0.80 us for only 128 elements. From its lines on POOL, 300 to 900 us:

```profile
L1047 POOL TENSOR_SCALAR xn<-x,mv,rstd 128x128 f32<-128x128 f32 x57 | 45.5, 799 | 10.4 <-POOL rstd L1044 10.4
```

  The Trainium skill, "GPSIMD Engine Reference", section "Elementwise — side-by-side cycle accounting", has 0.77 us for 512 elements as the best case of a tight loop; here the one-input instruction from float32 to float16 took 1.49, twice that, so this form is far from that best case.
- **What followed from it.** "`t.norm` starts up to 1.9 us earlier, if the split on POOL is done by then": it was not done, and `t.norm` stayed 2.0 late. With the split at 2.55 us it starts within 0.3 us of the statistics (e8). The diagnosis behind it was half right: of the two waits of the kernel before, that of `k.shift` was worth 0.5 us a period (p4), that of `t.norm` at most 0.13 (p1). In the new orders the late `t.norm` counts, since `k.eb` stands behind the tree's copies in ACT's table.
- **The new ring** held, as far as the runs with less or no split on POOL show it: 30.6 by hand, 30.70 measured with the split at its forecast size, and e2, f1, f2 lie above by what they put into it. `k.shift` went from 2.43 us of idle time to 1.24. The forecast of -33 us for the middle would have been about -29 (985.0 to 955.6 us from the first to the last `k.top`, before and in e8).
- **Rival 2** is in its second half what happened in the regular period: "the split at 4.6 us", "`t.norm` behind the split is late by as much", P 31.5. Its first half isn't: from 300 to 900 us PE has no wait for the keys. It had a chance of 0.13 and 1104 us; the profiled execution is 37 us above. Of these, 17 lie between tiles 3 and 30 (+13.3 us, where P = 31.5 gives 27 x -0.14 = -3.8), somewhat under half of them the longer iterations and the rest the regular 31.88. 5 lie before tile 3, 8 in the start (+3.6 instead of -4) and 8 in the end (+19.0 instead of +11).
- **Rival 1** didn't happen. L plus issue was taken as 7.2 + 1.0 = 8.2; from the start of an issue to the landing it is 7.8 us by the median beside the rest of the traffic, and 7.6 from one issue to the next in the quiet end (6.7 behind the issue's end). The issue took 0.93. The middle of two bounds was no more than a choice, and it came within 0.6 us. The Trainium skill's estimate in the prediction, 6.8 us, agrees with the 6.7 of the quiet end. POOL waits 2.7 us an iteration for them, more than the 2 named, at no cost (e3).
- **Rivals 3 and 4** didn't happen either: no kernel's period is below 30.5, and the issue holds POOL for 0.93 us and not for the DMA.
- **`k.kturn`.** The 1.1 us of slack was right for what the split takes (the keys landed in time in the middle), but the step looked at the landing alone in the regular iteration. In the last one `e.sc` no longer waits for anything and goes out 0.04 us ahead of the keys: 9.4 us instead of 3.1.
- **The end**: +11 forecast, +10.8 measured from the first mask on; +8.3 on top for the late keys. That the 11 came out is partly luck: the three DMAs took 22.2 us from the first issue to `e.fin` where 24.6 were forecast, `e.sa` went out 0.9 us later against the first mask than forecast, and 1.1 us came behind the last sum. **The start**: -4 forecast. The first `x.s0` came at 17.51, as forecast, 4.9 us earlier than before; but the first `k.top` came 3.6 us later in the profile, and 2 us earlier in those at full clock.
- What the split's size did in all is about the difference to e8: 1139.35 - 1085.55 = 54 us of the 64 by which the forecast was off. 3 us of it are the start, which the split doesn't explain.

## What to carry to other kernels

When work moves to another engine, price it from that engine's own row of the same form and scale it by the elements; where there is none, let the sum be made at the upper bound too, and see which step stands behind the moved one. Ahead of the head of a long chain a moved step that is too long costs something in every period, however idle its engine is otherwise: here 1.75 us more of split cost 1.2. And a DMA that is hidden in the middle is bare in the last tile: sum the last tile on the engines, and keep a large accumulating DMA from being issued ahead of a small one that others wait for, unless it will have landed by then.

## What the runs showed of the hardware

- A transposing DMA of the keys lands in 3.0 us without accumulating DMAs, mostly in 3.1 when it is issued 6.6 us or more behind the start of an accumulating 1 MB DMA (after, e8), in 3.3 to 6.2 us 4.9 to 7.1 us behind (p4), in 3.2 to 6.8 us 3.9 to 6.1 us behind (p1), and in 6.8 (e1, each iteration) or 9.4 us (the last tile of the changed kernel) 0.04 us behind one. Behind one of 16 KB it lands in 3.3 (e3).
- GpSimd takes 1.49 us for 512 elements from float32 to float16 and 0.85 for 256: 2.5 ns an element and 0.2 us besides. VectorE takes 0.43 for the 512. A two-input float32 addition of 2048 elements takes GpSimd 4.51 us, of 1024 elements 2.36.
- An accumulating DMA within SBUF of 1 MB costs GpSimd 0.93 us of issue and lands 7.0 us after it in the quiet end of the changed kernel, 7.6 to 8.5 us by the median of each kernel that has them at full size. Cut to 16 columns it lands after 2.6 us but costs 1.27 us of issue.
- In these kernels PE's granted clock fell to half for part of 3 to 11 of 27 iterations where PE's longest regular wait was 1.2 to 1.7 us, and of none to two where it was 0.8 to 1.0 us; what decides in a single iteration is open. In the start the same instructions ran at half clock in some profiles and at full clock in others.
